# Transposing the first node tile as twelve 64-row halves in two rounds instead of six whole transposes

## What is computed

```python
h = jnp.maximum(_layernorm(x, axis=-1), 0.0)
q = h @ wq.T + bq;  k = h @ wk.T + bk;  v = h @ wv.T + bv
q2 = (q @ wiq.T + biq).reshape(N, H, D).transpose(1, 0, 2)      # k2, v2 alike
scores = jnp.einsum('hnd,hmd->hnm', q2, k2) * scale + mask[None]
out = jnp.einsum('hnm,hmd->hnd', softmax(scores), v2).transpose(1, 0, 2).reshape(N, F)
return x + out @ wo.T + bo
```

## Time and profile before

| what | us |
|---|---|
| median of 3 runs | 299.58 (299.3 to 299.6) |
| the profiled execution, own time | 299.46 |
| its span, first to last instruction | 297.7 |
| TensorE busy | 291.4 (98%) |
| VectorE busy | 177.7 (60%) |
| ScalarE busy | 153.6 (52%) |
| GpSimd busy | 148.5 (50%) |
| TensorE's idle time after the warm matmuls, by the waits of PE | 1.1, in three places |

### The profile page before, as it was taken

How to read it: one execution, slowest core, us unless ns; L and a number is a source line. 1 busy time by engine, 2 the same in 40 slices (tenths; PEclk the granted TensorE clock), 3 DMA queues, 4 the chain that set the end, 5 groups by cost and what they waited for, 6 DMA issues and landing times.

```text
span 297.7 us, 4737 instructions
## 1 busy us (share of the span) xinstructions
PE 291.4 (98%) x1705; PEld 271.6 (91%) x1705; DVE 177.7 (60%) x475; ACT 153.6 (52%) x288; POOL 148.5 (50%) x153
## 2 busy tenths in 40 slices
PE   6999999999999999999999999999999999999996
PEld 3799998888899999999999999999999999888885
DVE  4995988786544443444467665656666666735241
ACT  2874642252532444334434586868686868975100
POOL 5551354643463545544400895657484839884000
PEclk9999999999999999999999999999999999999999
DMA  7948875648743444333554043040404040400032
GB/s 269 329 154 284 280 232 191 219 166 279 285 115 108 132 141 143 109 109 137 186 184 143 0 142 104 40 137 7 141 3 143 1 141 12 167 36 2 0 141 73
DMA packets 15818, 40.84 MB, mean 137 GB/s; under 512 B 3481, under 2 KB 4914, under 8 KB 15794
## 3 DMA queue, kind: packets, MB, share of 16 engines
q1 hardware_dynamic: 13346, 38.53, 38.9%
q0 software_dynamic: 2016, 1.21, 1.4%
q10 hardware_dynamic: 432, 0.79, 0.7%
HBM read 37.71 MB, written 2.81 MB: 136 GB/s over the span
## 4 chain that ended last, share of the span: by engine, by line
PE 89%; DMA 4%; DVE 3%; ACT 2%; issue 0%; POOL 0%; SPq 0%
PE bank L805 25%; PE bank L807 24%; PE bank L806 24%; PE bank L933 5%; PE bank L920 5%; PE bank L949 3%; PE bank L948 3%; DMA raw<-in_slabs 2%; DMA x_sb<-in_x 1%; ACT w_hi L433 1%; DVE stats L640 1%; ACT a_hi L463 1%; DMA key_rows<-key_row 1%; DVE a_lo L686 0%; ACT x_sb L453 0%
## 5 line engine op out<-in xcount | busy, mean ns | idle before, releaser
L386 POOL DMA_INDIRECT cells<-value,cell x51 | 53.1, 1042 | 63.8 <-DMA cells<-value,cell 46.8
L433 ACT ACTIVATE w_hi<-raw 128x1024 fp32r<-128x1024 f32 x51 | 54.1, 1060 | 22.2 <-PE bank L807 17.3
L805 PE MATMUL bank<-a_hi,w_hi 128*128 128x384 f32 x184 | 61.6, 335 | 0.7 <-DVE b_lo L661 0.7
L807 PE MATMUL bank<-a_lo,w_hi 128*128 128x384 f32 x184 | 61.5, 334 | 0.0
L806 PE MATMUL bank<-a_hi,w_lo 128*128 128x384 f32 x184 | 61.5, 334 | 0.0
L673 DVE TENSOR_TENSOR w_lo<-raw,w_hi 128x1024 fp32r<-128x1024 f32 x36 | 44.0, 1223 | 15.6 <-ACT w_hi L433 15.6
L412 POOL TENSOR_SCALAR prob<-prob,row_inv 128x384 f32<-128x384 f32 x36 | 22.7, 642 | 40.1 <-DVE row_inv L740 40.1
L357 POOL TENSOR_TENSOR w_lo<-raw,w_hi 128x1024 fp32r<-128x1024 f32 x15 | 35.9, 2395 | 7.1 <-ACT w_hi L433 7.1
L805 PEld LDWEIGHTS bank<-a_hi,w_hi 128*128 128x128 f32 x184 | 34.5, 188 | 1.1 <-DVE w_lo L673 1.0
L806 PEld LDWEIGHTS bank<-a_hi,w_lo 128*128 128x128 f32 x184 | 34.5, 188 | 0.0
L807 PEld LDWEIGHTS bank<-a_lo,w_hi 128*128 128x128 f32 x184 | 34.5, 188 | 0.0
(11 more groups left out here) (142 smaller groups left out, 609.2 us busy)
## 6 DMA issues: line engine op xcount, KB each, us to landing
raw<-in_slabs SPq DMA_DIRECT2D x56, 512.0 KB, 3.4
work<-key_rows SPq DMA_DIRECT2D x6, 256.0 KB, 6.2
prob<-key_rows SPq DMA_DIRECT2D x6, 256.0 KB, 3.8
x_sb<-in_x SPq DMA_DIRECT2D x3, 512.0 KB, 6.3
out_y<-x_sb SPq DMA_DIRECT2D x5, 256.0 KB, 2.1
cells<-prob SPq DMA_DIRECT2D x2, 576.0 KB, 7.4
cells<-value,cell POOLq DMA_INDIRECT x51, 3.8
x_sb<-in_x ACTq DMA_DIRECT2D x3, 256.0 KB, 4.4
```

What stands on the lines that cost most here:

```text
L386: nc.gpsimd.indirect_dma_start(out=cells[c][:, :], out_offset=bass.IndirectOffsetOnAxis(ap=cell[:, t:t + 1], axis=0), in_=value[:, t:t + 1 ...
L433: nc.scalar.activation(split_place(s)[0], raw[:, s % RAW, :], ACT.Copy).then_inc(slab_hi, 1)
L805: nc.tensor.matmul(psum, w[0], a[0], start=first, stop=False)
L807: return nc.tensor.matmul(psum, w[0], a[1], start=False, stop=last)
```

## The change

Only TensorE's stream and one semaphore change. For node tile 0, feature tiles 0 to 5 are no longer turned whole. Each is turned in two halves of 64 nodes (half of the rows of x_sb, all 128 features), x = 0 on rows 0 to 63 and x = 1 on rows 64 to 127, each with its own 64x64 corner of the identity and 64 columns of the bank. In round 0 the halves x = 0 take k = 0, 1, 2 and the halves x = 1 take k = 3, 4, 5; in round 1 the other way round. Neighbours in the stream thus lie on different rows and in different banks. Every half counts `half_turned`; round 1 waits for all 6 of round 0, and the stream waits for all 12 behind round 1. Feature tile 6 of node tile 0 stays a whole transpose, behind that wait. The 4 warm matmuls and all that follows stay.

```diff
-        h_turned, h_hi, h_lo = sem("h_turned"), sem("h_hi"), sem("h_lo")
+        half_turned, h_turned, h_hi, h_lo = sem("half_turned"), sem("h_turned"), sem("h_hi"), sem("h_lo")
...
             pe.wait_ge(ident_ok, 1)
+            def turn_h_in_halves(t):
+
+                for turn in range(2):
+                    if turn == 1:
+                        pe.wait_ge(half_turned, KT - 2)
+                    for i in range(NT):
+                        for x in range(2):
+                            k, own = i + NT * (turn ^ x), slice(x * D, (x + 1) * D)
+                            nc.tensor.transpose(h_bank[k][:, t * P + x * D:t * P + (x + 1) * D],
+                                                x_sb[own, t, k * P:(k + 1) * P], ident[own, own]).then_inc(half_turned, 1)
+                pe.wait_ge(half_turned, 2 * (KT - 2))
+
             for t in range(NT - 1):
                 pe.wait_ge(h_ok, t + 1)
-                for k in range(KT - 1):
+                if t == 0:
+                    turn_h_in_halves(t)
+                for k in range(KT - 2 if t == 0 else 0, KT - 1):
                     turn_h(k, t)
                 warm(WARM[t + 1])
```

## The result

Over 20 executions of each the changed kernel has a median of 300.72 us (299.19 to 303.96), the kernel before 299.59 us (298.91 to 303.49). The ratio is 1.0044, 95% interval [1.0025, 1.0063]: slower by 1.1 us between the medians, above the predicted range. Every ratio in this document is of fast runs alone: it leaves out executions more than 1.5% above the fastest of their kernel, and with them some of those with a late mask. The kernel before had shown three executions within 0.3 us; with 20 it shows that it, too, sometimes takes 300 to 303 us.

The account below looks back on a forecast made before the run. TensorE, busy 291.4 of 297.7 us, was taken as the bound. Node tile 0's block grows 0.35 us within 0.39 slack, so no delay: profiled 299.46 + 0 = 299.5, against the median 299.6 us; range 299.2 to 300.3.

Parts of the forecast that it names:

- Halves go two at a time: Node tile 0's half transposes run in pairs, as the 64-row score products do: three steps a round, not six; chance 0.72.
- A step: Time from one pair of half transposes to the next: 0.06 us, upper end 0.11.
- Leaving 64 rows: Going back to whole transposes behind round 1: no cost, as it lies inside the second wait; 0.10 us without that cover.
- D: Delay the change passes on from node tile 0's block: 2R − 0.94, zero if negative; forecast 0, upper ends with pairs 0.38 us.
- the wait of TensorE for itself: Each new wait behind a round of halves, for one semaphore: 0.05 us, upper end 0.11.
- R: Length of one round of halves: load 0.06, three steps of 0.06, 0.16 to the result, wait 0.05; 0.45 us.
- the way into 64 rows: Going from the warm matmuls to the first half transposes: loading at about 8.17 instead of 8.07, +0.10 us, lower bound 0.
- steps that follow their columns: Reason given for the halves' short step: 64 moving columns for 128 gives 0.055 us, taken as 0.06 for the weight load.
- Behind that TensorE waits for nobody: After TensorE's last wait, ending at 30.45 us, no other engine holds it up through the end of the kernel.
- my five rivals: Alternatives: halves unpaired with short steps (0.12) or full steps (0.07); the third rival (0.05); faster loads (0.04); colliding banks, counted under unpaired.
- My third rival: A slower TensorE clock in the opening, making the kernel slower; chance 0.05.
- along this chain to the end, one for one: A delay reaching node tile 2 at 11.18 us passes through copies, splits, key row and slab loads to the end undiminished.

Follow-up runs that it names:

- a_again2: A repeat of the changed kernel without further edits; its repeats measured 301.48, 301.89 and 300.74 us, and the text doesn't say which is this one.
- experiments 3, 4 and 6: Both kernels with each chain's last two scatters omitted (before 299.32, changed 299.22 us); mask building behind k_lo (299.47, 299.23); VectorE's slab splits halved (298.97, 299.30).
- experiment 8: Both kernels with VectorE's slab splits halved and mask building behind k_lo: before 298.98 us, changed 299.12 us; the changed kernel unedited again: 300.74 us.
- experiment 7: Kernel before, whole transposes for node tile 0, with two waits of TensorE for its own results put between them: 299.26 us, ratio 0.9985.
- b_warm7: Kernel before with 7 instead of 4 warm matmuls behind node tile 0, no halves: 302.15 us, ratio 1.0061.
- experiment 2: Warm matmuls behind node tile 0 altered from 4: to 7 in the kernel before (302.15 us, 1.0061), to 2 in the changed kernel (302.88 us, 1.0035).
- a_hold: Changed kernel with three warm matmuls put ahead of TensorE's fifth tile: 301.67 us, ratio 1.0067.

## Why the prediction was wrong

**Right, by its own steps.** The first half loads at 8.17 (8.17 foretold). Halves go two at a time. A step is 0.06. The last half ends 0.16 behind its step, as a whole transpose does. Leaving 64 rows cost nothing extra (0.50 us from the second round to feature tile 6, as from the first round to the second). Node tile 1 starts at 9.99 and node tile 2 at 11.24; D = 0.06 us in this execution for the 0 foretold, and 0 in most others. Two sizes are off. The first is the wait of TensorE for itself. R came out as 0.50, so the wait is what the load, three steps and the time to the result (0.06 + 3 × 0.06 + 0.16) leave of it, 0.10 us, twice the 0.05 that I took and inside its bound of 0.11. With R = 0.50 the formula 2R − 0.94 gives the 0.06. The second is the way into 64 rows: its 0.10 us shows only where the last warm matmul starts at 7.84 or 7.85, as it does here and in one more trace of the changed kernel (a_again2). In the other eight traces with halves the warm matmuls end earlier, and the first half loads 0.11 or 0.12 us behind ACT's end, as the whole transpose did (7.96 to 8.07), and there D is 0.

One reason was wrong though its size came out: steps that follow their columns. The 0.163 us of 384 columns and the 0.109 of 128 are 0.42 and 0.85 ns a column.

**Wrong, one step.** "Behind that TensorE waits for nobody", and with it "from the same cases": the sum, the rivals and the range were all built on the chain of one execution. In that execution the mask was in time, with 2.1 us to spare for TensorE. The timeline of DVE of the kernel before has k_lo there, done at 156.95, where the scores start at 159.01:

```profile
156.34 0.61 DVE L661 SCALAR_TENSOR_TENSOR k_lo<-bank,bias,k_hi 128x384 fp32r<-128x384 f32 x1
```

With the last scatter 2 to 4 us later there is a wait of 1.3 to 2.4 us at 160 us (six traces), and in three of the six a stretch at a granted clock of 0.50 behind it. None of my five rivals had that mechanism. It acts from outside the change: experiments 3, 4 and 6 take it away by three routes, experiment 8 by two of them together, and of their 94 executions none is over 301, whichever opening the kernel has.

My third rival, with its 0.05, was a slower TensorE clock in the opening, and no run shows one behind 8 us: in all ten traces with halves the granted clock is 1.00 up to 30 us, and the 384-column products at 14 us start 0.17 us apart. Ahead of that the 18 warm matmuls of the kernel before start 0.32 us apart (the first at 2.45, the last at 7.84), the later ones 0.163, and the page prints 1.00 for both. What makes the first ones slower is not shown.

The signs stood in the trace of before: VectorE itself waited 0.5 us for the mask, the mask hangs on two chains of 27 scatters each, and in VectorE's stream it stood ahead of k_lo. I had asked only what TensorE waits for.

**Also off: "along this chain to the end, one for one".** The 0.06 us at 11.2 had shrunk to 0.02 when SP went on (19.23 for 19.21): POOL started L395, a step of the key row, 0.09 us later, but took 1.21 us for it instead of 1.29. Then the slab issued at 21.26 rather than 21.25 landed 0.17 us sooner, and TensorE resumed at 30.28 instead of 30.45. Over the profiled executions that point moved between 29.7 and 30.6. A delay of 0.06 is below what the chain's own loads scatter by.

**What stays open.** Why the changed kernel has late masks more often: at least half of its executions, at least a fifth of those of the kernel before. It isn't the delay alone (experiment 7 had more of it: 2 of 12; b_warm7, experiment 2: 9 of 12) and not a need for halves (b_warm7 has none). In the fourteen traces the question is settled by 84 us: the 25th scatter starts at 81.6 to 82.6 us in the seven whose mask is in time, and at 83.4 to 86.5 in the seven with a late one. The hold-ups go part of the way. Those behind the splits add up to 7.0 to 8.4 us in the seven traces with halves and to 4.2 to 6.9 in the seven with whole transposes; but late and timely masks overlap in them (5.7 to 8.4 against 4.2 to 7.3), and how the opening would reach them is not shown. With 12 executions a kernel a share is known to some 15 points at best. That the change costs 1.1 us is measured; that 64-row transposes cost it is not.

## What to carry to other kernels

A change that costs the opening a tenth of a microsecond at most can come with a median ten times that higher, if somewhere a chain of another engine ends with little to spare: look through the waits of every engine for one that ends just ahead of what the bounding engine needs, and count its spare time before trusting a sum. Three executions don't show how often such a chain is late, and even twenty showed it once for the kernel before, where 187 had it in a fifth. Mending the margin (the consumer later in its stream, the blocking instruction cut in two) was worth more here, about 0.5 us of the median, than anything in the opening.

## What the runs showed of the hardware

- By the record matmuls overlap, so that the step from start to start is less than the length: a whole transpose lasts 0.273 us and the next one starts 0.109 us behind it, a product of 384 columns lasts 0.33 to 0.34 us and the next one starts 0.17 behind it.
- Transposes of fp32 in 64-row halves with 64 moving columns run two at a time, 0.06 us a pair, where a whole one costs 0.109. Their price here was going in (0.10 us, where matmuls ran right up to them) and two waits of TensorE for its own results (0.16 until the result, 0.10 until the next weight load).
- A scatter of GpSimd that starts within 1.09 us behind the start of a VectorE split of 128x1024 fp32 is held up by up to 1.0 us (2.00 instead of 0.96): in 269 of 269 cases it ended 2.04 to 2.08 us behind the split's start. The split keeps its 1.22 us, and a scatter that starts ahead of it its 0.96.
- One idle stretch of 1.8 us in TensorE's stream was followed, 0.9 us after it had resumed, by 3.4 us at a granted clock of 0.50, with steps of 0.32 us for 384 columns where they are 0.17 at 1.00. It doesn't always follow: in the profiled execution of a_hold TensorE waited 1.8 us at the same place, and the granted clock stayed at 1.00 and the steps at 0.17.
